# A gated two-layer block on one core: fewer weight units decoded ahead, another order of the first products, and token folds in the downs

## Chip, cores and metric

One core of a Trainium2 chip (trn2) runs the whole kernel. The metric is the device time of one execution in microseconds; the median of three runs is quoted.

## What is computed

Eight sequences of 256 tokens with 1024 features pass through four residual updates, each on a layer norm of the stream and scaled by the tanh of a gate: linear attention, a feed-forward net with 4-bit weights, an auto-correlation attention, and a linear layer with a column norm. The change touches the first two.

```python
x = x + tanh(g_xattn[0]) * linear_attention(layernorm(x), ctx, ctx)
x = x + tanh(g_ffn[0])   * ffn(layernorm(x))
x = x + tanh(g_xattn[1]) * autocorrelation(layernorm(x), ctx, ctx)
x = x + tanh(g_ffn[1])   * linear_with_norm(layernorm(x))

def ffn(x1):                    # DM = 1024, DFF = 2752, LoRA rank 16
    Wg, Wu, Wd = (NF4[codes] * absmax per block of 64, transposed)
    y1 = x1 @ Wg + x1 @ g_lora_a @ g_lora_b
    y2 = x1 @ Wu + x1 @ u_lora_a @ u_lora_b
    x3 = relu(y1) * y2
    return x3 @ Wd + x3 @ d_lora_a @ d_lora_b
```

## The kernel before, in words

**Phases.** `phase_linear_attention` (to 180 us of the span), `phase_nf4_ffn` (to some 1500 us), `phase_tail`. All engines run their own instruction lists in order and meet at semaphores. Matrices are split into a high and a low float16 part; a product is three matmuls (high x high, high x low, low x high).

**Linear attention.** Sixteen tiles of 128 tokens, one step each, with a few steps of lead and tail. In a step ScalarE copies transposed exponentials (L440), runs kinks of weight decoding (`first_kinks`, L424, instructions L434), spreads reciprocals (L446), takes the next tile's two exponentials (L413, L417), copies a PSUM tile (L452), normalises (L459) and casts a transposed tile (L422). POOL multiplies (L395) and computes reciprocal square roots (L386, L388). VectorE, among others, scales them (L525), makes the low half of a transposed tile (L539) and the reciprocal of sums (L549).

**Decoding.** The feed-forward weights come in units of 128 x 512 four-bit codes, as int32. A unit is decoded by eight Prelu operations on ScalarE in place, one per kink of a piecewise linear function. `AHEAD = 6` units are decoded in the linear attention: steps 1 to 8 run the eight kinks of units 0 to 2, one kink of each per step, and steps 9 to 16 those of units 3 to 5. Later ones go through `decode` (L1028), in two parts of four operations (instructions L1036).

**The feed-forward net.** DFF is padded to eleven pairs of two 128-row chunks c = 0, 1; a pass j handles a pair. A pass has gate and up products (A11, A12 are the two halves of the gate weights of a chunk, A21, A22 those of the up weights), then 32 downs, which multiply the hidden values with the down weights D0 to D3 and add into the stream X. Pass 0 does its products straight from the token tiles; from pass 1 on, products follow Strassen's scheme with seven products of combined operands. Their token combinations T1 to T4 are made once, in pass 0, for each of eight batches i (`fold_begin` on POOL L1309, two operations; `fold_first` L1658, three, and `fold_second` L1669, four, on VectorE; four casts `fold_hi` L1112, instructions L1118, on ScalarE; four `fold_lo` L1319, instructions L1323, on POOL), stored to DRAM (`x_parts`) and loaded back tile by tile.

**Steps of pass 0.** It has 24 steps, and every engine has a list for each (`first_step` at L1153 ScalarE, L1325 POOL, L1681 VectorE). Steps 0 to 15 are products: `first_products(n, m)` with s = 2n + m is 24 matmuls, for gate (m = 0) or up (m = 1) of turn n. `turn(n)` (L744) gives group g of tokens, chunk c, row half r. Turn n may begin when the hidden product of turn n - 2 is made (`hidden_first`, L1651, instruction L1656), since it takes over its PSUM banks. Steps 16 to 23 have four downs each. The 32 downs share six PSUM banks, and each waits until VectorE has accumulated the one that had its bank (`accumulate`, L1497, instruction L1501); the downs 4 and 5 wait for the last hidden product.

The list of VectorE in a step is short, and its order matters:

```python
if 0 < s <= 2 * TURNS and m == 1: hidden_first(n)
if folding(s): (fold_first, fold_second)[part](i)
for n in ...: accumulate(0, n)            # from step 16 on, four
for w in ended(0, s): weights(w)          # and lora_parts(1) after unit 11
```

ScalarE: ReLU of the turn (even m), a half decode, cast of units that ended a step before (`w_hi`, L1039, instruction L1055), cast of the hidden (odd m), casts of the fold, a second half decode where `halves` (L717) gives two. POOL: low parts of units (`w_lo`, L1255, instruction L1265), of the hidden (L1332), then the next batch's `fold_begin` and the low parts of the fold. `weights` (L1418) is two VectorE operations (L1439, L1442) and, for units of the next pass, one or two sums. `lora(w)` (L1730) is a small matmul in TensorE's order.

`halves(0, s)` is 1 in steps 0 to 15 and 1, 2, 1, 2, ... from 16 on; the units 6 to 19 are decoded there. `folding(s)` puts the two parts of batch i into steps 2i + 1 and 2i + 2, the last one into step 16. Units 0 to 3 are chunk 0, 4 to 7 chunk 1, 8 to 11 the downs of pass 0, 12 to 19 the gate and up units of pass 1.

**SyncE** issues all loads in order: per unit that ends, the load of unit w + 3 (L896), which waits until unit w has been scaled; the stores of folds; in step 18 the loads of token tiles 0 and 1 for pass 1, in step 20 those of tiles 2 to 4 (L909).

Of the kernel before, what the change touches and what calls it, by code (L numbers as in the profile page):

```python
# [20 lines left out]
I32 = mybir.dt.int32  # L21
# [6 lines left out]
B, L, D = 8, 256, 1024  # L28
# [13 lines left out]
HALVES = 2  # L42
UNITS = 12
CH = BANK // P
AHEAD = 6
LROWS = 96
GROUPS = 2
PRODUCTS = 7
# [528 lines left out]
def phase_nf4_ffn(nc, io, res):  # L577
# [11 lines left out]
    RING = 3  # L589
# [5 lines left out]
    TURNS = 4 * GROUPS  # L595
# [4 lines left out]
    with ExitStack() as ctx:  # L600
# [4 lines left out]
            return ctx.enter_context(nc.semaphore(name))  # L605

        lead = [res["first"][:, u, :] for u in range(AHEAD)]
        codes = [t.bitcast(I32) for t in lead[AHEAD - RING:AHEAD]]
        absm = [res["absm"][:, s, :] for s in range(RING)]
        level = lead[0:2]  # L610
        wt = [res["wt"][:, s, :] for s in range(4)]
# [102 lines left out]
        def steps(j):  # L714
            return ups(j) + DOWNS

        def halves(j, s):  # L717

            if j == 0:
                return 2 if s >= 2 * TURNS and s % 2 else 1  # L720
            if j == LAST_PASS:
                return 1 if s < 8 else 0
            return 2 if s in (14, 17) else 1
# [8 lines left out]
        def ended(j, s):  # L732

            return [w for w, part in decoded(j, s) if part]

        def earlier(j, s):

            return ended(j, s - 1) if s else ended(j - 1, steps(j - 1) - 1) if j else [4, 5]

        def sequence(j, g, p):  # L740

# [1 line left out]

        def turn(n):  # L744

            return n // 4, n // 2 % 2, n % 2

        def first_product(n, m):

# [29 lines left out]

        def all_hid(j, g):  # L780

            return (2 * j + g) * 4 + 4

        def folding(s):


            i, part = divmod(s - 1, 2)
            return (i, part) if 0 <= i < B else None

        def begun(i):  # L790

# [55 lines left out]
        for w in range(8 + LAST_PASS * UNITS + 4):  # L847
            j, u = unit_at(w)
# [44 lines left out]
        with nc.Block() as block:  # L893
            @block.sync
            def _(sp):
# [64 lines left out]
                for s in range(FIRST_STEPS):  # L960
                    if folding(s - 1):
                        i, part = folding(s - 1)
                        for k in range(2):
                            store_part(4 * i + 2 * part + k)
                    loads(0, s)
                    if 3 <= s < 3 + 3 * GROUPS:
                        store_block(s - 3)
                    if s == 2:
                        load_lora(1)
                    if s == 18:  # L970
                        for c in range(2):
                            sp.wait_ge(prod_mm[c], 4)
                        sp.wait_ge(blocks_out, 16 * 3 * GROUPS)
                        wait_parts(16)
                        for t in range(2):
                            load_x(t)
                    if s == 20:
                        for c in range(2):
                            sp.wait_ge(prod_mm[c], 8)
                        wait_parts(4 * B)  # L980
                        for t in range(2, XRING):
                            load_x(t)
                    if s == FIRST_STEPS - 1:
                        sp.wait_ge(hidlo_done, all_hid(0, 1))
                        for dst, name in zip(l_f, ("lora1_a", "lora1_b")):
                            sp.dma_start(dst, io[name]).then_inc(l_in, 16)
                for j in range(1, PAIRS):
                    if j < LAST_PASS:
                        load_lora(j + 1)
                    for s in range(steps(j)):  # L990
                        t = (j - 1) * UPS + s - 1 + XRING
                        if 0 < s <= UPS and t < LAST_PASS * UPS:
                            g, p = divmod(s - 1, PRODUCTS)
# [735 lines left out]
            def _(pe):  # L1729
                def lora(w):  # L1730


                    j, u = unit_at(w)
                    m, c, hf = units[u]
                    if u == 0:
                        pe.wait_ge(lb_done, j + 1)
                    if j == 0 and u in (0, 2, 8):
                        pe.wait_ge(la_done, m + 1)
                    if w > 1:
                        pe.wait_ge(wt_done, w - 1)  # L1740
                    o = ps_lora[w % 2]
                    if m == 2:
                        mm = pe.matmul(o[:], lora_b[:, m, c * P:(c + 1) * P], lora_a[:, m, hf * BANK:(hf + 1) * BANK], start=True, stop=True)
                    else:
                        for k in range(KD // 2):
                            kk = hf * (KD // 2) + k
                            mm = pe.matmul(o[:, k * P:(k + 1) * P], lora_a[:, m, kk * P:(kk + 1) * P], lora_b[:, m, c * P:(c + 1) * P], start=True, stop=True)  # L1747
                    mm.then_inc(lora_mm, 1)
# [193 lines left out]
                for s in range(FIRST_STEPS):  # L1942
                    if s < 2 * TURNS:
                        first_products(*divmod(s, 2))
                        if s == 0:
                            lora(4)
                            lora(5)
                        side(0, s)
                    else:
                        downs(0, s - 2 * TURNS)  # L1950
                for j in range(1, PAIRS):
                    for s in range(steps(j)):
                        g, p = divmod(s, PRODUCTS)
# [672 lines left out]
def build(nc, io):  # L2626
    with ExitStack() as ctx:
# [18 lines left out]
        for name, shape in (("a_st", [P, 2, 12]), ("a_mv", [P, 2, 2]), ("a_ve", [P, 2]), ("a_rstd", [P, 2]), ("a_nmr", [P, 2]),  # L2646
                            ("top8", [P, CH, 8]), ("next3", [P, CH, 8]), ("nmax", [P, CH]), ("wsum", [P, CH]), ("rws", [P, CH])):
            res[name] = sb(name, shape)
        for name, n in (("first", AHEAD), ("absm", 3), ("wt", 4)):
            res[name] = sb(name, [P, n, BANK])  # L2650
        res["made"] = sb("made", [P, 2, BANK], HALF)
        res["o_sp"], res["k_sp1"] = sb("o_sp", [P, 2, BANK]), sb("k_sp1", [P, 2, BANK])
# [122 lines left out]
```

## Time and profile before

| | |
|---|---|
| median of 3 runs | 2003.04 us (2002.95 to 2003.74) |
| the profiled execution, its own time | 2003.48 us |
| its span, first to last instruction | 2001.5 us |
| TensorE busy | 1918.8 us (96%) |
| VectorE busy | 1293.8 us (65%) |
| ScalarE busy | 1254.9 us (63%) |
| POOL busy | 835.4 us (42%) |

The profile gives for one execution the busy time of each engine, its idle time before an instruction with what released it, and a timeline. PE is TensorE's matmul, PEld its weight load, DVE VectorE, ACT ScalarE, SP SyncE. L12 is line 12 of the kernel. Matmuls overlap in the records: one of 512 columns shows 0.38 us, but a new one begins every 0.22 us at full clock.

### The profile page before, as it was taken

How to read it: one execution, taken by the hardware profiler on the slowest of the kernel's cores; microseconds unless marked ns; L12 is line 12 of the kernel's file. 1: busy time of each engine (PE TensorE's matmuls, PEld its weight loads, DVE VectorE, ACT ScalarE, POOL GpSimd, SP SyncE). 2: the span in 40 equal slices, each digit the busy share in tenths (PEclk: the TensorE clock that was granted, in tenths of full speed). 3: DMA queues.
4: the chain of work that ended last, by engine and by line, in shares of the span. 5: the costliest groups of instructions: out<-in, count | busy, mean ns of one | idle time of the engine just before them, and what ended most of it. 6: DMA issues, size and time to landing. Idle time of an engine off the chain costs nothing. (4 is left out here: it accounts for less than half of the span.)

```text
span 2001.5 us, 26467 instructions
## 1 busy us (share of the span) xinstructions
PE 1918.8 (96%) x9140; PEld 963.6 (48%) x9140; DVE 1293.8 (65%) x2204; ACT 1254.9 (63%) x1998; POOL 835.4 (42%) x752
## 2 busy tenths in 40 slices
PE   6996888999999999999999999999998899999998
PEld 5774334444444444444444445444444455555554
DVE  5776888364564736555473644636379988888872
ACT  6995668886777677676777776677524343443431
POOL 2443884222223223232232333222268667667742
PEclk9997998999999999999999999999999999999999
DMA  5651545856637375573737556373531110111001
GB/s 201 223 171 55 193 163 195 292 193 215 232 122 265 105 257 190 178 249 127 265 109 252 192 172 227 99 253 117 210 137 59 32 41 29 53 53 38 27 22 42
DMA packets 91989, 303.01 MB, mean 151 GB/s; under 512 B 11984, under 2 KB 16720, under 8 KB 73168
## 3 DMA queue, kind: packets, MB, share of 16 engines
q1 hardware_dynamic: 91856, 301.32, 44.3%
q8 instruction: 73, 1.20, 0.2%
q14 instruction: 60, 0.49, 0.1%
HBM read 274.01 MB, written 27.26 MB: 151 GB/s over the span
## 5 line engine op out<-in xcount | busy, mean ns | idle before, releaser
L1036 ACT ACTIVATE first<-first 128x512 f32<-128x512 int32 x1008 | 625.7, 626 | 27.4 <-DVE wt L1439 1.8
L1265 POOL TENSOR_TENSOR gu<-wt,gu 128x512 f16<-128x512 f32 x86 | 102.3, 1190 | 370.6 <-ACT gu L1055 370.5
L1439 DVE SCALAR_TENSOR_TENSOR wt<-first,w_scale,absm 128x512 f32<-128x512 f32 x132 | 102.6, 777 | 227.4 <-ACT first L1036 226.8
L1785 PE MATMUL a_psQ<-z,gu 128*128 128x512 f16 x936 | 208.5, 379 | 0.0
L2386 PE MATMUL a_psL<-z,l_x 128*128 128x512 f16 x768 | 170.7, 379 | 1.0 <-DVE l_x L2488 0.8
L1785 PE MATMUL a_psC<-z,gu 128*128 128x512 f16 x732 | 167.8, 379 | 0.0
L1785 PE MATMUL a_psC<-z 128*128 128x512 f16 x684 | 156.9, 379 | 0.0
L1785 PEld LDWEIGHTS a_psQ<-z,gu 128*128 128x128 f16 x936 | 91.5, 98 | 110.5
L1277 POOL TENSOR_TENSOR hid_lo<-z,hid_hi 128x512 f16<-128x512 f32 x76 | 90.2, 1201 | 118.7 <-ACT hid_hi L1096 118.6
L1265 POOL TENSOR_TENSOR dn_lo<-wt,dn_hi 128x512 f16<-128x512 f32 x42 | 50.3, 1197 | 199.2 <-ACT dn_hi L1055 199.2
L1442 DVE SCALAR_TENSOR_TENSOR wt<-a_psE,lora_gain,wt 128x512 f32<-128x512 f32 x132 | 99.1, 751 | 44.6 <-PE a_psE L1747 24.4
L2386 PEld LDWEIGHTS a_psL<-z,l_x 128*128 128x128 f16 x768 | 74.9, 98 | 89.1 <-issue 1.2
L1265 POOL TENSOR_TENSOR z<-wt,z 128x512 f16<-128x512 f32 x57 | 66.4, 1179 | 119.4 <-ACT z L1055 119.4
L1785 PEld LDWEIGHTS a_psC<-z,gu 128*128 128x128 f16 x732 | 70.7, 98 | 82.3
L1055 ACT ACTIVATE gu<-wt 128x512 f16<-128x512 f32 x86 | 53.4, 622 | 89.7 <-DVE wt L1442 78.5
L1501 DVE SCALAR_TENSOR_TENSOR X<-a_psL,ffn_gain,X 128x512 f32<-128x512 f32 x132 | 94.9, 744 | 19.8 <-PE a_psL L1838 19.7
L1785 PEld LDWEIGHTS a_psC<-z 128*128 128x128 f16 x684 | 66.4, 98 | 78.8
L1838 PE MATMUL a_psL<-dn_hi,hid_hi 128*128 128x512 f16 x268 | 101.6, 379 | 1.4 <-DVE X L1501 1.4
L1785 PE MATMUL a_psL<-z 128*128 128x512 f16 x456 | 101.7, 379 | 0.0
L1838 PE MATMUL a_psL<-dn_hi,hid_lo 128*128 128x512 f16 x268 | 101.5, 379 | 0.0
L1501 DVE SCALAR_TENSOR_TENSOR X<-a_psQ,ffn_gain,X 128x512 f32<-128x512 f32 x106 | 77.8, 746 | 36.8 <-PE a_psQ L1838 36.8
L1501 DVE SCALAR_TENSOR_TENSOR X<-a_psC,ffn_gain,X 128x512 f32<-128x512 f32 x108 | 78.6, 746 | 31.1 <-PE a_psC L1838 30.9
(418 smaller groups left out, 4122.3 us busy)
## 6 DMA issues: line engine op xcount, KB each, us to landing
z<-x_parts SPq DMA_DIRECT2D x140, 1024.0 KB, 5.8
first<-in_codes SPq DMA_DIRECT2D x132, 256.0 KB, 3.0
absm<-in_absmax SPq DMA_DIRECT2D x264, 128.0 KB, 3.3
X<-in_x SPq DMA_DIRECT2D x16, 512.0 KB, 4.3
c_in<-in_ctx SPq DMA_DIRECT2D x16, 512.0 KB, 5.3
cT<-in_ctxT SPq DMA_DIRECT2D x16, 512.0 KB, 3.6
o_sp<-in_w SPq DMA_DIRECT2D x16, 512.0 KB, 4.8
z<-in_ctx SPq DMA_DIRECT2D x8, 1024.0 KB, 7.0
```

What stands on the lines that cost most here:

```text
L1036: act.activation(level[w % 2][:], codes[w % RING] if k == 0 else level[w % 2][:], ACT.Prelu, bias=bias, scale=scale, alpha=alpha).then_inc ...
L1055: act.activation(dest(c, name, 0), wt[slot(name)], ACT.Copy).then_inc(whi_done, 1)
L1265: pool.tensor_tensor(low, source, high, ALU.subtract).then_inc(wlo_done, 1)
L1277: pool.tensor_tensor(low, buf, high, ALU.subtract).then_inc(hidlo_done, 1)
L1439: dve.scalar_tensor_tensor(wt[at], source[:], w_scale[:, m:m + 1], absm[w % RING][:], ALU.mult, ALU.mult).then_inc(scaled, 1)
L1442: dve.scalar_tensor_tensor(wt[at], ps_lora[w % 2], lora_gain[:, m:m + 1], wt[at], ALU.mult, ALU.add).then_inc(wt_done, 1)
L1501: dve.scalar_tensor_tensor(dst, ps_ring[down_bank(j, n)], ffn_gain[:], dst, ALU.mult, ALU.add).then_inc(acc_done, 1)
L1785: mm = pe.matmul(out, w[:, k * P:(k + 1) * P], xx[:, k], start=first and q == 0, stop=q == 3 * KD // 2 - 1, skip_group_check=True)
L1838: mm = pe.matmul(ps_ring[down_bank(j, n)], hh[c][:, i * P:(i + 1) * P], w[c][:, hf * BANK:(hf + 1) * BANK], start=(q == 0), stop=(q == len ...
L2386: mm = pe.matmul(sum_bank(d, half), a[:, ks], w[:, k, half * CB:(half + 1) * CB], start=(q == 0), stop=(q == 3 * KD - 1))
```

## The change

Four units instead of six are decoded in the linear attention, two in steps 1 to 8 and two in steps 9 to 16; units 4 to 19 are decoded in pass 0, two halves in steps 6 and 12 and from 18 on. The buffer `first` keeps six slots, and codes of later units use slots 3 to 5. The turns of pass 0 run over all tokens with chunk 0 and then with chunk 1. The parts of the folds lie in two of three steps up to 14 and in steps 16 to 21. The loads of tiles 2 to 4 move from step 20 to step 22, and the LoRA matmuls of units 4 and 5 from step 0 to steps 1 and 3.

```diff
-AHEAD = 6
+AHEAD = 4
+FIRST_SLOTS = 6
...
-        codes = [t.bitcast(I32) for t in lead[AHEAD - RING:AHEAD]]
+        codes = [res["first"][:, u, :].bitcast(I32) for u in range(FIRST_SLOTS - RING, FIRST_SLOTS)]
...
         def halves(j, s):
             if j == 0:
-                return 2 if s >= 2 * TURNS and s % 2 else 1
+                return 2 if s in (6, 12) or s >= 18 else 1
...
         def earlier(j, s):
-            return ended(j, s - 1) if s else ended(j - 1, steps(j - 1) - 1) if j else [4, 5]
+            return ended(j, s - 1) if s else ended(j - 1, steps(j - 1) - 1) if j else []
...
         def turn(n):
-            return n // 4, n // 2 % 2, n % 2
+            return n // 2 % 2, n // 4, n % 2
...
         def all_hid(j, g):
-            return (2 * j + g) * 4 + 4
+            return (2 * j + g) * 4 + 4 if j else 6 + 2 * g
...
         def folding(s):
-            i, part = divmod(s - 1, 2)
-            return (i, part) if 0 <= i < B else None
+            order = [t for t in range(1, 16) if t % 3] + list(range(16, 22))
+            return divmod(order.index(s), 2) if s in order else None
...
-                    if s == 20:
+                    if s == 22:
                         for c in range(2):
                             sp.wait_ge(prod_mm[c], 8)
                         wait_parts(4 * B)
...
                     if s < 2 * TURNS:
                         first_products(*divmod(s, 2))
-                        if s == 0:
-                            lora(4)
-                            lora(5)
                         side(0, s)
...
-        for name, n in (("first", AHEAD), ("absm", 3), ("wt", 4)):
+        for name, n in (("first", FIRST_SLOTS), ("absm", 3), ("wt", 4)):
```

## Rows read from the trace of the kernel before

**Rows 1.** Busy time by stretch: start:end, length, busy and count per engine, TensorE clock, DMA.
```profile
75.00:175.00 100.00, 85.41 (x582) 68.90 (x580) 74.14 (x151) 88.39 (x111) 39.43 (x49) 0.98 0.44 144
203.00:304.00 101.00, 81.99 (x367) 35.84 (x365) 85.86 (x80) 65.44 (x114) 84.51 (x60) 0.93 0.49 176
346.30:446.30 100.00, 100.00 (x483) 45.98 (x482) 48.67 (x70) 80.61 (x138) 27.69 (x25) 1.00 0.72 241
```
**Rows 2.** Timeline of TensorE, pass 0: start, length, instruction, [idle before, releaser].
```profile
200.81 10.53 PE L1806 MATMUL a_psC<-z,gu 128*128 128x512 f16 x48
...
227.50 4.97 PE L1806 MATMUL a_psQ<-z,gu 128*128 128x512 f16 x12 [6.91 <-POOL gu L1265]
...
278.01 0.40 PE L1747 MATMUL a_psE<-lora_b,lora_a 96*128 96x128 f16 x4 [3.02 <-DVE lora_b L1416]
...
304.67 0.61 PE L1838 MATMUL a_psC<-dn_hi,hid_hi 128*128 128x512 f16 x1 [8.24 <-DVE gain_row L1656]
...
311.21 0.39 PE L1838 MATMUL a_psL<-dn_hi,hid_hi 128*128 128x512 f16 x1 [1.24 <-DVE X L1501]
...
346.25 5.34 PE L1785 MATMUL a_psQ<-z,gu 128*128 128x512 f16 x24
```
**Rows 3.** Timeline of ScalarE, POOL and VectorE in one step of the linear attention.
```profile
87.18 1.00 ACT L452 ACTIVATE wt<-psB 128x1024 f32<-128x1024 f32 x1
...
91.08 1.66 ACT L434 ACTIVATE first<-first 128x512 f32<-128x512 f32 x3
93.27 1.06 ACT L446 ACTIVATE wt<-made 128x1024 f32<-128x1024 f32 x1 [0.52 <-DVE made L549]
...
88.26 2.36 POOL L395 TENSOR_TENSOR eq<-wt,eq 128x1024 f32<-128x1024 f32 x1 [0.44 <-ACT wt L452]
...
91.49 0.16 DVE L525 SCALAR_TENSOR_TENSOR made<-made 128x1 f32<-128x1 f32 x1 [0.79 <-POOL made L388]
...
92.83 0.34 DVE L549 RECIPROCAL made<-psB 128x32 f32<-128x32 f32 x1
```
**Rows 4.** Timeline of ScalarE: L446 in steps 2 and 15.
```profile
37.35 1.05 ACT L446 ACTIVATE wt<-made 128x1024 f32<-128x1024 f32 x1
...
160.25 1.05 ACT L446 ACTIVATE wt<-made 128x1024 f32<-128x1024 f32 x1
```
**Rows 5.** Timeline of VectorE in pass 0.
```profile
211.85 0.74 DVE L1656 SCALAR_TENSOR_TENSOR gain_row<-a_psQ,hid_gain,gain_row 128x512 f32<-128x512 f32 x1
...
242.82 1.52 DVE L1679 TENSOR_TENSOR first<-first,z 128x512 f32<-128x512 f32 x1
...
248.10 0.75 DVE L1439 SCALAR_TENSOR_TENSOR wt<-first,w_scale,absm 128x512 f32<-128x512 f32 x1 [0.86 <-ACT first L1036]
...
252.14 0.69 DVE L1673 TENSOR_TENSOR o_sp<-o_sp,z 128x512 f32<-128x512 f32 x1 [1.84 <-POOL k_sp L1323]
...
303.87 0.74 DVE L1656 SCALAR_TENSOR_TENSOR gain_row<-a_psC,hid_gain,gain_row 128x512 f32<-128x512 f32 x1
...
344.62 1.40 DVE L1501 SCALAR_TENSOR_TENSOR X<-a_psC,ffn_gain,X 128x512 f32<-128x512 f32 x2
```
**Rows 6.** Timeline of ScalarE in pass 0.
```profile
196.66 2.62 ACT L1036 ACTIVATE first<-first 128x512 f32<-128x512 int32 x4 [1.40 <-DMA first<-in_codes]
...
245.40 2.60 ACT L1036 ACTIVATE first<-first 128x512 f32<-128x512 f32 x4
...
249.24 0.63 ACT L1118 ACTIVATE k_sp<-o_sp 128x512 f16<-128x512 f32 x1 [0.72 <-DMA x_parts<-k_sp]
```
**Rows 7.** Timeline of POOL in pass 0.
```profile
249.83 2.28 POOL L1323 TENSOR_TENSOR k_sp<-o_sp,k_sp 128x512 f16<-128x512 f32 x2
252.97 1.61 POOL L1265 TENSOR_TENSOR dn_lo<-wt,dn_hi 128x512 f16<-128x512 f32 x1 [0.86 <-ACT dn_hi L1055]
```
**Rows 8.** SyncE's timeline in pass 0, then the DMA issues of the page (count, size, us to landing).
```profile
329.55 1.42 SPq L909 DMA_DIRECT2D z<-x_parts  x3
...
z<-x_parts SPq DMA_DIRECT2D x140, 1024.0 KB, 5.8
```

## The prediction

> **What bounds the kernel now.** I read the busy time by stretch first, then each engine in order of time where the change touches it. From 346.3 us on TensorE has no idle time [rows 1]: whatever moves the start of pass 1 (346.25 us, [rows 2]) moves the end by as much. So the question is when pass 0 ends. Two stages come before. In the first phase (to 180 us) ScalarE looks like the bound, busy 88 of 100 us [rows 1]. In pass 0 TensorE waits 6.91, 3.02 and 8.24 us [rows 2], each time for work of the other three engines, and VectorE is idle only 15.1 of 101 us [rows 1].
>
> **First phase: one kink fewer per step (L424).** Is ScalarE's kink work on the path? In one step ScalarE ends its three kinks and then still waits 0.52 us for the reciprocal L549 [rows 3]. Follow that wait back: L549 follows L525, which waits for POOL's L388, which stands behind the product L395 (2.36 us), which waits for ScalarE's L452 at 87.18 [rows 3]. From L446 on ScalarE runs without idle to the next L452. This ring makes the step of 9.3 us, and the kinks lie beside it: without one of them (1.66 / 3, some 0.5 us) the wait becomes 1.0 us and nothing is gained. Only in steps 2 and 15 does L446 start right behind the kinks, with no wait shown [rows 4]: 2 x 0.5 = **-1.0 us**. Bounds: 0, and 16 x 0.5 = -8.3 if my ring is wrong.
>
> **How pass 0 is costed.** TensorE does a product turn (two steps) in 10.6 us [rows 2], sixteen steps in 85. I lay out VectorE, ScalarE and POOL in the order of their step lists: an operation starts when its engine is free and its wait is met. Prices: half a decode 2.6 us on ScalarE, a cast 0.55; on VectorE a unit's weights 1.5 (two operations of 0.75), a hidden product 0.7, an accumulation 0.66 in a row; a combination operation 0.69 alone and 1.53 while POOL runs [rows 5, 6]; on POOL 1.15 alone, 1.6 beside VectorE [rows 7]. I write h0 to h7 for the hidden products L1656, which TensorE waits for two turns later; the last two feed the downs.
>
> **Start of pass 0.** The 1.40 us wait for codes [rows 6] goes, since the codes of unit 4 are asked for two units earlier, and two casts of units 4 and 5 leave (1.1 us). h0, which ended at 212.6 [rows 5], ends at 209.8. The weights of units 4 and 5 (3.0 us of VectorE) and four decode halves (10.4 us of ScalarE) come in behind it. The 6.91 us wait for the low part of unit 7 goes: chunk 1 is first needed in step 8, not 4. What is late next is the hidden product of two turns before.
>
> **Steps 2 to 16 by hand.** Steps 2 and 3: combination ends 213.4; ScalarE has by then decoded only half of unit 5, its second half ends 217.2; weights, then h1 at 219.4. Steps 4 and 5: first combination to 222.3; in POOL's list the low parts of unit 5 and of h1 (3.0), the next batch's two first operations (2.4) and two low parts (2.3) stand ahead of the second combination, so VectorE waits until 228.1, 5.8 us with nothing in its list between (before, weights and a hidden product stood there and 1.84 us was left [rows 5]). Second combination 231.4, weights 233.6, h2 at 234.3: TensorE, ready at 232.2, waits 2.1. Steps 6 to 9: unit 7 is ready only at 238.3 (two halves and two casts from 232.0), weights 239.8, combination 241.9, h3 242.6; wait for POOL to 248.0; combination 252.5, weights, h4 at 255.4. So six steps take 36 us against TensorE's 31.8. Steps 10 to 12: combination 258.0, unit 9 ready at 259.3 and its weights 260.9, wait for POOL to 266.0, combination 270.5, h5 at 271.2 (TensorE, ready at 267.2, waits 4.0). Steps 12 to 16: both halves of unit 10 or 11 fall into step 12, so its list is one half longer; unit 10's weights 275.2, combination 277.5, unit 11's weights 281.4, the next pass's LoRA rows some 284.0, h6 at 284.7; POOL's low parts to 286.9, combination 290.9; ScalarE then has two casts, a ReLU and half of unit 12, to 294.5; weights 296.0, h7 **296.7**, where it was 304.6 [rows 5]. The low half of D3 (unit 11), decoded only in step 13, is ready at 288.1, so the downs start there, not at 291.1; they stop at the fifth for h7. Products thus gain 8 us.
>
> **The downs.** Three batches now lie here (21 combination operations, before 4), in VectorE's list ahead of each step's accumulations, and TensorE can run only six banks ahead of those. From h7 to accumulation 25, which frees the bank of the last down, VectorE has 21 combinations (at 1.1, midway, since POOL has work for about half of that stretch, 25 operations of 1.15: 23), 26 accumulations (17.2), weights of units 13 to 17 (7.5), five sums (3.5), and waits for POOL's low parts in the first pair (some 4): 55.6 us. So accumulation 25 ends at 352.3, the last down 1.5 us later, 353.8 against 346.25: **+7.5 us**. Bounds: all 21 at 0.69 (-8.6), all at 1.53 (+9.0). ScalarE keeps up: 10 halves, 12 and 9 casts are 37.6 us there.
>
> First the row: combinations take 0.69 or 1.53 us, and POOL's operations 1.15 or 1.6, as the other runs or not [rows 5, 7]. The Trainium skill, SBUF — State Buffer, "SBUF: two separate sides", says why: a VectorE operation with two SBUF inputs and a GpSimd operation take an exclusive lock in turn, and the loser blocks for the whole instruction. By that rule the stretch from h7 to accumulation 25 holds 25 POOL operations (28.8 us) and 31 such VectorE operations (21.4), 50.2 us at least, so an end of pass 0 at 348.4 even with every other wait gone; put in place of the 55.6 it gives 2004.6 us. The trace agrees in the two values that each operation takes.
>
> **Pass 1.** SyncE's load of tiles 2 to 4 moves from step 20 to 22, and there it stands behind unit 21's load, which waits for unit 18's first scaling (some 355). Before, it was issued at 329.55 [rows 8]. Issue at 357 and 5.8 us to landing, three side by side some 7: 364, and product 2 wants them at 364.4. I take **+0.5 us**; bounds 0 and 3. Loads of tiles 0 and 1 keep step 18, and the folding of tokens 0 to 3 ends in step 11, well ahead. all_hid(0, 0) = 6 costs nothing: h5 ends 17 us before the downs.
>
> **Sum.** -1.0 + 7.5 + 0.5 = +7.0 us on the profiled execution (2003.48 us, span 2001.5). That execution is 0.44 above the median of the runs shown, which I take as the base: 2003.0 + 7.0 = **2010.0 us**. A measurement of this kernel tells some 0.2%, 4 us, from no change.
>
> **Rivals.**
> Faster: the waits of VectorE do not grow. Its work up to accumulation 25 is the same but for units 4 and 5; my layout is longer by some 14 us of waits, most of them at the second combination. If POOL gets through the two first operations of the next batch (2.4 us) while VectorE is still in its own three, that gap shrinks by 2.4 in five product batches and in the first downs pair: 14.4 us, 1995.6. It decides from 1.2 us per batch on. For it: POOL is relieved of a third of its folds, 84.5 us busy in 101 [rows 1]. Against: low parts of units and hiddens stand ahead of them, behind ScalarE's decodes. Chance 0.27, from 1994 to 1999.
> No difference: ScalarE does bound the first phase, as its 88% suggest; all sixteen steps shrink, 7.3 us more than in the sum: 2002.7. Against: the 0.52 us wait in every steady step. With the cases that end between the two others by chance, 0.22.
> Slower still: TensorE's clock. After its 6.91 us of waiting, 12 matmuls took 4.97 us, twice the usual [rows 2], the half clock of 1.2 GHz. If it stays there through downs that starve, a step of 24 takes 9.9 us, and 28 downs 69 instead of 57: 2022. The Trainium skill, TensorE: Matmul & The Clock Gate, Part 1, calls the throttled clock the default that activity releases. Against: in the first phase the granted clock is 0.98 with TensorE busy 85 of 100 us [rows 1]. Chance 0.06.
> Forecast, slower: 0.45.
>
> **Numbers.** The forecast's own range, 2006 to 2018, comes from the price of combinations in the downs and from h7 5 us earlier or later. With the faster rival the range is 1994 to 2020. Faster 0.27, same 0.22, slower 0.51.
>
> **What would show it.** Right: first-phase step still 9.3 us with the wait before L446 near 1.0; no TensorE wait for a low part of chunk 1 around step 5; h7 near 296; TensorE in the downs waiting for X (L1501) again and again, where it waited 1.24 us once [rows 2]; VectorE near 90% busy from 297 to 352; pass 1 beginning near 353. Wrong: a first-phase step of 8.8 us; or VectorE waiting under 2 us at each second combination and pass 1 beginning before 346; or TensorE waiting for z at product 2 by more than 3 us.

## The result, and the profile after

The changed kernel takes **2027.87 us** (median of 4 runs, 2025.03 to 2030.49), the kernel before 2003.39 beside it (4 runs); ratio 1.0119, 95% interval 1.0101 to 1.0136. Slower by 24.5 us: the forecast's side, but 17.9 us above 2010.0 and outside the range. The profiled execution took 2030.49 us (span 2028.7, against 2001.5). Code lines of the feed-forward part are one higher than before (L1656 is now L1657).

Busy time of the changed kernel by stretch, columns as in [rows 1]. The second line runs from the first hidden product to the last (h0 to h7), the third from the start of h7 to the end of accumulation 25:

```profile
75.00:175.00 100.00, 85.89 (x575) 68.86 (x574) 73.40 (x150) 82.50 (x100) 39.45 (x49) 0.96 0.43 144
208.73:297.73 89.00, 77.55 (x343) 33.77 (x341) 49.05 (x58) 61.97 (x107) 50.01 (x42) 0.92 0.50 181
297.73:360.98 63.25, 41.07 (x183) 17.71 (x184) 50.10 (x65) 38.47 (x66) 34.30 (x26) 0.87 0.39 123
363.20:463.20 100.00, 93.56 (x440) 42.36 (x439) 46.02 (x65) 77.91 (x133) 27.59 (x24) 0.97 0.78 263
```

The products are shorter (h0 to h7 took 92.0 us before), the downs much longer: the third stretch took 36.0 us before. Pass 1, whose first 100 us were 100% busy [rows 1], now has 6.4 us without TensorE.

TensorE's timeline in the changed kernel, which answers to [rows 2]:

```profile
243.31 2.76 PE L1807 MATMUL a_psQ<-z,gu 128*128 128x512 f16 x12 [1.19 <-POOL gu L1266]
...
271.34 13.16 PE L1807 MATMUL a_psC<-z,gu 128*128 128x512 f16 x48 [3.89 <-DVE gain_row L1657]
...
311.57 0.61 PE L1839 MATMUL a_psC<-dn_hi,hid_hi 128*128 128x512 f16 x1 [3.91 <-DVE X L1502]
...
331.82 0.61 PE L1839 MATMUL a_psL<-dn_hi,hid_hi 128*128 128x512 f16 x1 [6.97 <-DVE X L1502]
...
345.24 0.61 PE L1839 MATMUL a_psC<-dn_hi,hid_hi 128*128 128x512 f16 x1 [6.43 <-DVE X L1502]
...
363.21 5.34 PE L1786 MATMUL a_psQ<-z,gu 128*128 128x512 f16 x24
...
385.65 4.56 PE L1786 MATMUL a_psC<-z 128*128 128x512 f16 x12 [6.43 <-ACT z L1074]
```

Pass 1 starts at 363.21, 17.0 us later than at 346.25 [rows 2]. From its start to the end of the span are 1665.5 us (2028.7 - 363.21), where they were 1655.3: 10.2 more. The two make the span's 27.2. In the downs TensorE waits again and again for X, that is for VectorE's accumulations. What does VectorE wait for? Its timeline there:

```profile
297.73 0.74 DVE L1657 SCALAR_TENSOR_TENSOR gain_row<-a_psC,hid_gain,gain_row 128x512 f32<-128x512 f32 x1
...
306.99 0.69 DVE L1674 TENSOR_TENSOR o_sp<-first,z 128x512 f32<-128x512 f32 x1 [2.99 <-POOL k_sp L1324]
...
322.39 1.20 DVE L1440 SCALAR_TENSOR_TENSOR wt<-first,w_scale,absm 128x512 f32<-128x512 f32 x1 [1.20 <-ACT first L1037]
...
339.37 0.75 DVE L1440 SCALAR_TENSOR_TENSOR wt<-first,w_scale,absm 128x512 f32<-128x512 f32 x1 [5.63 <-ACT first L1037]
...
348.40 0.75 DVE L1440 SCALAR_TENSOR_TENSOR wt<-first,w_scale,absm 128x512 f32<-128x512 f32 x1 [1.25 <-ACT first L1037]
...
357.40 0.75 DVE L1440 SCALAR_TENSOR_TENSOR wt<-first,w_scale,absm 128x512 f32<-128x512 f32 x1 [1.21 <-ACT first L1037]
...
359.58 1.40 DVE L1502 SCALAR_TENSOR_TENSOR X<-a_psL,ffn_gain,X 128x512 f32<-128x512 f32 x2
...
362.93 0.75 DVE L1440 SCALAR_TENSOR_TENSOR wt<-first,w_scale,absm 128x512 f32<-128x512 f32 x1 [0.63 <-ACT first L1037]
```

Accumulation 25 is the second of the pair at 359.58. Four of the five units' weights before it wait for ScalarE's kinks (9.3 us in all), the longest 5.63. One step further back, ScalarE's timeline (L1119 is the cast of a folded part into one of three stage buffers, which must first have been stored to DRAM):

```profile
319.15 0.63 ACT L1119 ACTIVATE k_sp<-o_sp 128x512 f16<-128x512 f32 x1 [2.23 <-DMA x_parts<-k_sp]
319.69 5.10 ACT L1037 ACTIVATE first<-first 128x512 f32<-128x512 f32 x8
...
328.01 0.63 ACT L1119 ACTIVATE made<-o_sp 128x512 f16<-128x512 f32 x1 [1.01 <-DVE o_sp L1676]
336.10 0.63 ACT L1119 ACTIVATE k_sp<-o_sp 128x512 f16<-128x512 f32 x1 [7.46 <-DMA x_parts<-k_sp]
336.64 5.10 ACT L1037 ACTIVATE first<-first 128x512 f32<-128x512 f32 x8
...
354.13 0.63 ACT L1119 ACTIVATE k_sp<-o_sp 128x512 f16<-128x512 f32 x1 [2.20 <-DMA x_parts<-k_sp]
...
383.88 1.05 ACT L1135 ACTIVATE o_sp<-gain_row 32x1024 f32<-32x1024 f32 x1 [7.07 <-DMA k_sp<-in_lora_b]
```

Two things are to be seen. The eight kinks (5.10 us) start each time right behind the two casts, so what holds a cast holds the next weights. And the casts wait for stores: 2.23, 7.46, 1.83 (at 345.14) and 2.20, together 13.7 us. Why is a store late? SyncE's timeline:

```profile
323.61 0.33 SPq L903 DMA_DIRECT2D first<-in_codes  x1
323.99 1.11 SPq L905 DMA_DIRECT2D absm<-in_absmax  x2
325.36 0.85 SPq L910 DMA_DIRECT2D z<-x_parts  x2
326.25 1.57 SPq L949 DMA_DIRECT2D x_parts<-k_sp  x2
...
365.38 1.40 SPq L910 DMA_DIRECT2D z<-x_parts  x3
...
372.06 0.60 SPq L987 DMA_DIRECT2D gain_row<-in_lora_a  x1
372.69 0.43 SPq L987 DMA_DIRECT2D k_sp<-in_lora_b  x1
```

The stores of 326.25 (256 KB each) stand behind a unit's load, which waits for a `scaled` of VectorE, and behind tiles 0 and 1, 2 MB; the cast is let go at 336.10, 9.9 us after their issue. Their usual time to landing, and that of the factor rows behind tiles 2 to 4 (3 MB), stands in the DMA view of 300 to 400 us (KB each, median us to landing):

```profile
x_parts<-k_sp SPq DMA_DIRECT2D x8, 256.0 KB, 3.4
...
gain_row<-in_lora_a SPq DMA_DIRECT2D x1, 384.0 KB, 8.8
k_sp<-in_lora_b SPq DMA_DIRECT2D x1, 384.0 KB, 11.2
```

The rows asked for at 372.69 let ScalarE go at 383.88, and behind L1135 on ScalarE stands the snapshot L1074 that TensorE waits 6.43 us for. (A snapshot is ScalarE's copy of a product out of PSUM, which frees the bank.) The 12 matmuls after that wait took 4.56 us at a granted clock of 0.58; in a4_folds_back (below) they took 2.75 us, at 1.00, after a wait of 0.51 us.

### The profile page after: what moved, and what is told of

Same layout as the page of the kernel before. It is cut to its first block and busy times, and to the rows that moved or that the text cites. A ratio compares the mean times of both kernels' runs of the same rounds, so it can differ in the third digit from the quotient of the medians.

```text
span 2028.7 us, 26469 instructions
## 1 busy us (share of the span) xinstructions
PE 1928.5 (95%) x9140; PEld 966.4 (48%) x9140; DVE 1277.7 (63%) x2204; ACT 1256.1 (62%) x1998; POOL 824.4 (41%) x752
## 5 line engine op out<-in xcount | busy, mean ns | idle before, releaser
L1037 ACT ACTIVATE first<-first 128x512 f32<-128x512 f32 (+1 forms) x1024 | 635.4, 626 | 26.3 <-DVE wt L1440 1.8
L1266 POOL TENSOR_TENSOR gu<-wt,gu 128x512 f16<-128x512 f32 x86 | 103.8, 1207 | 385.8 <-ACT gu L1056 385.8
L1266 POOL TENSOR_TENSOR dn_lo<-wt,dn_hi 128x512 f16<-128x512 f32 x42 | 48.7, 1160 | 209.5 <-ACT dn_hi L1056 209.5
L1839 PE MATMUL a_psL<-dn_lo,hid_hi 128*128 128x512 f16 x254 | 97.8, 385 | 0.0
```

The lines of the kernel that those rows point to most:

```text
L1037: act.activation(level[w % 2][:], codes[w % RING] if k == 0 else level[w % 2][:], ACT.Prelu, bias=bias, scale=scale, alpha=alpha).then_inc ...
L1266: pool.tensor_tensor(low, source, high, ALU.subtract).then_inc(wlo_done, 1)
L1839: mm = pe.matmul(ps_ring[down_bank(j, n)], hh[c][:, i * P:(i + 1) * P], w[c][:, hf * BANK:(hf + 1) * BANK], start=(q == 0), stop=(q == len ...
```

## The experiments

Theory A: the folds in the downs cost what they cost because ScalarE's casts wait for late stores; the factor rows behind tiles 2 to 4 are a second cost, of its own. Rival B: two more units decoded in pass 0 are the loss. C and D came later. All results in one table: median; first to last hidden product; last hidden product to accumulation 25 (the downs); start of pass 1; from there to the end of the span. "4" and "6" are the units decoded ahead.

```
                     median   h0-h7  downs  pass 1   rest
before (6)          2003.39    92.0   36.0  346.25  1655.3
after (4)           2027.87    89.0   63.3  363.21  1665.5
b6_order            2004.38    92.4   36.0  345.45  1655.3
b6_order_folds      2019.52    82.4   57.6  355.64  1660.5
a4_folds_back       2009.39   105.1   38.7  355.15  1657.7
a4_factors_first    2020.33    89.2   63.1  360.26  1657.3
a4_tiles_early      2022.50    88.7   58.1  357.45  1662.3
a4_stores_now       2021.01    88.7   57.2  354.75  1664.1
a4_both             2014.00    88.7   58.4  358.92  1655.8
a4_sums_first       2033.56    88.8   69.8  371.19  1662.6
a4_casts_last       2019.53    89.7   56.2  355.48  1661.8
a4_cure             2013.47    88.7   57.1  358.69  1655.2
a4_cure_casts       2012.03    88.7   54.7  354.36  1657.0
a4_cure_short       2002.91    88.6   45.4  345.71  1656.3
b6_cure             2006.84    94.3   37.7  349.22  1656.9
a4_cure_back        2010.16   103.8   38.7  350.58  1656.9
b6_folds_cure       2006.98    81.7   53.2  349.07  1655.9
a4_mix_cure         2007.11    91.8   47.8  346.19  1656.3
b6_mix_cure         2003.01    85.9   42.0  345.60  1655.2
```

The median is the result; the stretches are of one execution, whose start to first product differs by some 2 us either way between kernels with the same first phase. That of a4_folds_back took 2014.61 us, 5.2 above its median. The kernel before, measured beside each group of kernels, had medians from 2003.39 (beside the result) to 2005.24 us (beside the next four), so a difference between kernels of two groups can be off by some 2 us.

### The change in parts

**a4_folds_back**: the changed kernel with the old folding steps and tiles 2 to 4 loaded at step 20 again.

```diff
-            order = [t for t in range(1, 16) if t % 3] + list(range(16, 22))
-            return divmod(order.index(s), 2) if s in order else None
+            i, part = divmod(s - 1, 2)
+            return (i, part) if 0 <= i < B else None
```

> The changed kernel, but with the folds in steps 1 to 16 and the loads of tiles 2 to 4 in step 20, as before. Theory A (the folds in the downs are what costs: VectorE waits for them with accumulations behind, and the late tile loads hold up the factor rows): pass 1 begins between 346 and 352 us instead of 363.2, no 6.4 us wait in pass 1, 2002 to 2009 us. Rival B (the two units decoded in pass 0 cost it, 10.4 us of ScalarE): pass 1 still begins after 357 us, 2014 to 2022.

2009.39 us, ratio 1.003 (1.0017 to 1.0043): almost as theory A expected. Pass 1 began at 355.15 in its profiled execution, between what A and B expected. **b6_order**: the kernel before with the new order only.

```diff
-            return n // 4, n // 2 % 2, n % 2
+            return n // 2 % 2, n // 4, n % 2
...
-            return (2 * j + g) * 4 + 4
+            return (2 * j + g) * 4 + 4 if j else 6 + 2 * g
```

> The kernel before with only the order of the turns changed (chunk 0 over all tokens first). Both theories: the 6.9 us wait for unit 7 goes, but the hidden products stay bound by VectorE's list, so h7 stays within 3 us of 304.6 and the time within 4 us of 2003. A third theory C, that the order itself costs (the last downs' hidden products crowd at the end), expects more than 2008.

2004.38 us, ratio 0.9996 (0.9987 to 1.0006): the order alone is free. Its trace loses the 6.91 us wait of [rows 2], and pays it back in four waits for hidden products (0.9 to 2.5 us) and 1.1 us more at the LoRA rows. **b6_order_folds**: the same with the new folding steps and later tiles.

```diff
-            i, part = divmod(s - 1, 2)
-            return (i, part) if 0 <= i < B else None
+            order = [t for t in range(1, 16) if t % 3] + list(range(16, 22))
+            return divmod(order.index(s), 2) if s in order else None
...
-                    if s == 20:
+                    if s == 22:
```

> Six units decoded ahead as before, new order of turns, folds spread into the downs and tiles 2 to 4 loaded in step 22. Theory A: nearly the whole loss is there, 2018 to 2026 us, with a wait for the factor rows in pass 1 above 4 us. Rival B: without the two extra units the loss is under half, 2003 to 2012.

2019.52 us, 1.0076 (1.006 to 1.0093). So folds in the downs cost 15.1 us with six units ahead and 18.5 with four (2027.87 - 2009.39); four units ahead cost 5 us with the old folds and 8.4 with the new. Set against the kernel before beside each, the 18.5 and the 8.4 are some 2 us larger. Either way the folds are the larger part, B the smaller.

**a4_factors_first**: the two factor loads (L987) at step 22, ahead of tiles 2 to 4, not in the last step.

```diff
                         wait_parts(4 * B)
-                        for t in range(2, XRING):
-                            load_x(t)
-                    if s == FIRST_STEPS - 1:
                         sp.wait_ge(hidlo_done, all_hid(0, 1))
                         for dst, name in zip(l_f, ("lora1_a", "lora1_b")):
                             sp.dma_start(dst, io[name]).then_inc(l_in, 16)
+                        for t in range(2, XRING):
+                            load_x(t)
```

> The changed kernel with the two loads of factor rows (lora1_a, lora1_b) issued in step 22 ahead of the loads of tiles 2 to 4, not after unit 22's load in step 23. Theory A2 (ScalarE's 7.1 us wait for these rows and TensorE's 6.4 us behind it come from 3 MB of tiles ahead of them in the queues): the wait in pass 1 falls under 1 us and the slow clock after it goes, 2018 to 2021 us. Rival: the snapshots are late anyway since ScalarE is behind at the end of pass 0, then 2025 to 2028.

2020.33 us: -7.5. The rows asked for second land 5.8 us after their issue, not 11.2. The 6.43 us wait in pass 1 is gone, the rest of the span is 1657.3 instead of 1665.5, the downs are as long as before.

### The stores

**a4_tiles_early** and **a4_both** (the same with the factors first):

```diff
-                    if s == 18:
+                    if s == 15:
```

> The changed kernel with tiles 0 and 1 of pass 1 (two loads of 1 MB) issued three steps earlier on SP (step 15, not 18), ahead of the downs instead of in their third step. Theory A (ScalarE's fold casts wait for stores of parts that stand behind those 2 MB and SP's unit load, and the downs' accumulations stand behind the folds): the wait of 7.46 us at 336 us falls to about 2, the two long waits of TensorE for X (6.97 and 6.43 us) lose about 6 us together, pass 1 starts at 356 to 359 us instead of 363.2, and the time falls by 4 to 7 us, to 2021 to 2024. Theory B (the folds' own work on VectorE, ScalarE and GpSimd is the length of the downs, stores only take the blame): pass 1 starts where it did and the time stays within 2 us of 2028.

> The changed kernel with tiles 0 and 1 issued at step 15 and the two factor loads of pass 1 issued ahead of tiles 2 to 4. If the two costs are separate (stores behind tiles 0 and 1 in the downs; factor rows behind tiles 2 to 4 in pass 1) they add: 7.5 us as measured with the factors alone, and the 4 to 7 us of the tiles: 2013 to 2017. If the one only moved the other's wait, the time is that of the better of the two alone, about 2020.

2022.50 and 2014.00: -5.4 and -13.9, which is the sum of the two within 1 us. **a4_stores_now** stores a part in the step that makes it, ahead of that step's unit load:

```diff
-                    if folding(s - 1):
-                        i, part = folding(s - 1)
+                    if folding(s):
+                        i, part = folding(s)
```

> The changed kernel with SP storing the parts of a fold in the step that makes them and ahead of that step's unit load, where they now wait for the step's unit load in the queue. Theory A has two causes for a late store: the queue's unit load ahead of it, and the bytes ahead of it. If the queue matters, ScalarE's three waits of about 2 us go, with 2 to 4 us of the time; the 7.46 us behind tiles 0 and 1 stays. If bytes alone matter, the time stays within 1 us of 2028. It can also turn slower, where SP's wait for a fold delays a unit load and with it a decoded unit.

2021.01: -6.9, more than the 2 to 4 expected, and no wait of ScalarE for a store is left in the downs. The expectation had the 7.46 us wait stay; but the move takes its store ahead of tiles 0 and 1 too (issued at 318.24, the tiles at 321.65), so for this wait the run does not part the place in the queue from the bytes ahead. The other three, 6.3 us in all, had only a unit's load in front: for them the place in SyncE's queue was enough. Yet the downs still took 57.2.

**a4_sums_first** puts `accumulate` ahead of the fold in VectorE's step of the downs.

```diff
+                    for n in range((s - 2 * TURNS) * PER_STEP, (s - 2 * TURNS + 1) * PER_STEP) if s >= 2 * TURNS else ():
+                        accumulate(0, n)
                     if folding(s):
...
-                    for n in range((s - 2 * TURNS) * PER_STEP, (s - 2 * TURNS + 1) * PER_STEP) if s >= 2 * TURNS else ():
-                        accumulate(0, n)
```

> The changed kernel with VectorE's accumulations of a downs step ahead of the fold part of that step, not behind it. Theory A (the accumulations are late because they stand behind folds that wait for ScalarE and the stores): TensorE's waits for X shrink to that of the first step or so, accumulation 25 ends 8 to 12 us earlier than 361.0, and the time falls by 5 to 10 us even though every store is as late as before; what can remain is that tiles 2 to 4 are loaded later, as the folds end later. Theory B (VectorE's own work in a step is what counts, in whatever order): acc 25 within 2 us of 361 and 2026 to 2030 us.

2033.56, 5.7 **slower**: the expectation fell, and with it the thought that accumulations are late because they stand behind folds. ScalarE's timeline in this kernel:

```profile
318.27 0.63 ACT L1119 ACTIVATE k_sp<-o_sp 128x512 f16<-128x512 f32 x1 [2.93 <-DVE o_sp L1662]
321.39 0.63 ACT L1119 ACTIVATE k_sp<-o_sp 128x512 f16<-128x512 f32 x1 [2.49 <-DVE o_sp L1668]
321.93 5.10 ACT L1037 ACTIVATE first<-first 128x512 f32<-128x512 f32 x8
```

Casts now wait for folds that stand behind the accumulations, and the kinks start that much later. It is a ring: weights (VectorE), folds (VectorE), casts (ScalarE), kinks (ScalarE), weights. An accumulation ahead of the folds lies in the ring, behind them beside it. In the trace the step from one unit's weights to the next grew from 9.0 us (339.37, 348.40, 357.40) to 11.5 and 11.2 (341.25, 352.77, 364.01), most of the 2.8 us of accumulations moved; the time grew by less than all such steps, since ScalarE's waits for stores fell from 13.7 to 5.0 us. This is theory C.

**a4_casts_last** opens the ring on ScalarE:

```diff
+                    for w, part in pieces[1:] if s >= 2 * TURNS else ():
+                        decode(w, part)
                     if folding(s):
...
-                    for w, part in pieces[1:]:
+                    for w, part in pieces[1:] if s < 2 * TURNS else ():
```

> The changed kernel with ScalarE's two fold casts of a downs step behind that step's kinks, not ahead of them. The trace of the changed kernel shows a ring in the downs: VectorE's weights wait for ScalarE's 8 kinks (5.10 us), the kinks stand behind two casts, the casts behind VectorE's folds, and the folds behind VectorE's weights: 9.0 us from one step's weights to the next where no store is badly late (339.37, 348.40, 357.40), against 5.5 in the step without a fold (357.40, 362.93). Theory C (that ring is a cost of its own, beside the late stores): with the kinks ahead, a step takes 7 to 8 us, ScalarE's waits for stores fall beside VectorE's folds, and the time falls by 4 to 9 us, to 2019 to 2024. Theory A alone (only the late stores stretch the downs): the stores are as late, and the time stays within 2 us of 2028.

2019.53: -8.3, downs 56.2, with SyncE's order untouched. ScalarE still waits 5.4 us for one store, but VectorE's waits for the kinks up to accumulation 25 fell from 9.3 to 0.8 us. So the late stores hurt mainly through the kinks behind them. **a4_cure** is all three moves on SyncE, **a4_cure_casts** those and the casts behind the kinks.

> The changed kernel with all three moves on SP: parts stored in their own step, tiles 0 and 1 at step 15, factor loads ahead of tiles 2 to 4. Tiles and factors together gave 2014.0, stores alone 7 us of 2028. The tiles and the stores take away the same waits in part (ScalarE's stores waited 13.7 us in all, of which the tiles' move left 6.1): theory A expects 4 to 5 us more than the two moves, 2009 to 2010.5, with no wait of ScalarE for a store in the downs. What is left over the kernel before (some 5 to 6 us) is then the ring of folds, kinks and weights, and fewer units decoded ahead.

> The three moves on SP, and the casts behind the kinks. Theory C: 3 to 6 us less than with the three moves alone, 2003 to 2007, near the kernel before. Without C: the same as the three moves alone, within 2 us.

2013.47 and 2012.03: both miss, and prompt stores on top of a4_both (2014.00) give nothing that the measurement can tell. The cures of the downs do not add: early tiles, prompt stores and late casts each take away the same 5 to 7 us, and below some 55 us the downs do not go. VectorE in the last of these kernels:

```profile
333.29 0.69 DVE L1459 TENSOR_TENSOR wt<-wt 128x512 f32<-128x512 f32 x1
333.90 0.68 DVE L1663 TENSOR_TENSOR first<-first,z 128x512 f32<-128x512 f32 x1
334.61 1.53 DVE L1667 TENSOR_TENSOR o_sp<-z,first 128x512 f32<-128x512 f16 x1
336.17 1.53 DVE L1669 TENSOR_TENSOR o_sp<-o_sp,z 128x512 f32<-128x512 f32 x1
337.63 1.40 DVE L1503 SCALAR_TENSOR_TENSOR X<-a_psC,ffn_gain,X 128x512 f32<-128x512 f32 x2
338.95 1.39 DVE L1503 SCALAR_TENSOR_TENSOR X<-a_psL,ffn_gain,X 128x512 f32<-128x512 f32 x2
340.27 0.73 DVE L1441 SCALAR_TENSOR_TENSOR wt<-first,w_scale,absm 128x512 f32<-128x512 f32 x1
```

No gap between one step's weights and the next, and none from 306.12 to 351.53. **a4_cure_short** tests that VectorE is the bound (theory D): the 21 combinations of the downs work on 32 columns of 512, and the rest of them is left out, so this kernel computes something else.

```diff
-                        (fold_first, fold_second)[part](i)
+                        (fold_first, fold_second)[part](i, 32 if s >= 2 * TURNS else BANK)
```

> As the three moves on SP and the casts behind the kinks, but VectorE's 21 fold instructions of the downs work on 32 of 512 columns (so tokens' combinations are left out in part; this only measures). Theory D (VectorE's own work bounds the downs of that kernel: busy 50.8 of 54.7 us, without a gap from 306.1 to 351.5): 21 instructions lose about 0.6 us each, and more where they took 1.5; the downs fall by 12 to 16 us to some 40 us, where ScalarE's 5.5 to 7 us a step take over, and the time to about 1998 to 2000. If something else bounds them, the downs shorten by less than 5 us.

2002.91: -9.1 us, downs 45.4, above the 1998 to 2000 and the some 40 expected. VectorE is busy 39.6 us there, 11.2 less than the 50.8 before, and the downs are 9.3 shorter: D holds. The gain is smaller than expected, since a wait of 4.48 us for POOL and some dear short combinations stay (below). **b6_cure** is the kernel before with the factors first and tiles 0 and 1 earlier:

```diff
-                    if s == 18:
+                    if s == 11:
```

> The kernel before with tiles 0 and 1 loaded seven steps earlier and the factor loads ahead of tiles 2 to 4. There no part is stored in the downs, TensorE is busy all through the first 100 us of pass 1, and ScalarE's only wait that these loads could cause is 2.4 us at the factors: both theories expect no measurable change, 2001 to 2005. Tiles 0 and 1 ahead of the stores of the last parts could cost 1 to 3 us.

2006.84, ratio 1.0009 (0.9999 to 1.0018): above the expected 2001 to 2005, and nothing to win there.

### What is left, and a split

**a4_cure_back** is a4_folds_back with the three moves on SyncE, **b6_folds_cure** is b6_order_folds with these and late casts. **a4_mix_cure** is a4_cure_casts with three fold parts in the downs, not six:

```diff
-            order = [t for t in range(1, 16) if t % 3] + list(range(16, 22))
+            order = [t for t in range(1, 16) if t not in (6, 12)] + list(range(16, 19))
```

> Four units ahead with the folds back in the products' steps and the three moves on SP. Folds back alone: 2009.4, downs 38.7 us, products 105 us from first to last hidden product (before 92). If late stores also stretched its products (ScalarE waited 17.5 us for them there), the time falls to 2004 to 2007; if four units ahead is the whole of its loss, it stays at 2008 to 2010.

> Six units ahead, the new order, folds in the downs, and all moves of the cured kernel (stores, tiles, factors, casts). Without them it was 2019.5. Theory D gives downs near VectorE's busy time (48.4 us plus some 3) where they were 57.6, and 3.4 us less in pass 1: 2007 to 2011. So folds in the downs alone would cost 3 to 6 us over the kernel before.

> The cured kernel with three fold parts in the downs instead of six: three more in steps 3, 9 and 15 of the products. Theory D: the downs lose 3 times VectorE's 2.9 to 4.5 us, some 10 us; the products gain 3 parts' share (six parts cost them 16 us between the two layouts: some 8 us). Time 2008 to 2012, near the cured kernel's 2012.

2010.16, 2006.98 and 2007.11 (ratios 1.003, 1.0013, 1.0012); the last is 0.9 below its expected range. The first says that four units ahead with the folds back lose nothing by late stores: ScalarE waited 17.5 us for them in a4_folds_back, none here, and the time is the same. With the cures, folds in the downs cost 1.9 us with four ahead (2012.03 - 2010.16), which is within the intervals of the two, and nothing with six (2006.98 against 2006.84), where they cost 18.5 and 15.1 without. Four units ahead cost 3.3 us with the folds back (2010.16 against b6_cure's 2006.84) and 5.1 with the folds in the downs. Three fold parts in the downs have the lowest median with four ahead; **b6_mix_cure** is the same with six:

> Six units ahead, new order, the moves on SP and the casts behind the kinks, three fold parts in the downs (six in b6_folds_cure, 2007.0; none before, 2004.4). If the optimum lies between, as with four ahead (3 to 5 us below both ends), 2000 to 2003 and faster than the kernel before. If VectorE's and ScalarE's work in these two stretches is the limit in whatever split, 2004 to 2007.

2003.01 against 2004.07, ratio 0.9995 (0.9986 to 1.0004): level with the kernel before, not faster, and at the edge of the 2000 to 2003 that a best split in between would have given.

## Why the prediction was wrong, point by point

**First phase: right.** The step is still 9.32 us, and ScalarE's wait behind the kinks is the predicted 1.0:

```profile
83.22 1.06 ACT L447 ACTIVATE wt<-made 128x1024 f32<-128x1024 f32 x1 [1.05 <-DVE made L550]
92.54 1.06 ACT L447 ACTIVATE wt<-made 128x1024 f32<-128x1024 f32 x1 [1.05 <-DVE made L550]
```

ScalarE's busy share fell from 88 to 82.5%, and hardly anything was gained by it. The first product starts at 185.7 us in the mean of the 13 kernels with four units ahead (183.5 to 187.8) and at 186.7 in the mean of the 6 with six: -1.0, the predicted term, though within the spread of single executions. The rival by which ScalarE bounds this phase is out.

**Products: right.** The hidden products ended at 209.5, 219.4, 233.9, 242.9, 254.8, 271.3, 284.4 and 298.5; the layout by hand had 209.8, 219.4, 234.3, 242.6, 255.4, 271.2, 284.7 and 296.7. (The layout leaves out the first phase's -1.0 us, which the sum adds on its own; with it h7 was forecast at 295.7 and pass 1 at 352.8.) VectorE's waits for POOL at the second combination were 5.63, 4.97, 4.85 and 2.49 us, where the layout had 5.8, 5.4, 5.1 and 2.2, and the wait for unit 7's low part shrank from 6.91 to 1.19 us. The faster rival, which lived on POOL getting through its list in time, is out. The low half of D3 came at 288.0 (288.1).

**Downs: the first step that failed.** From the end of h7 to accumulation 25 it took 62.5 us, not 55.6. VectorE's own work was sized rightly: the 21 combinations took 21.5 us (1.02 each, 1.1 predicted), weights 8.0 (7.5). Wrong was "ScalarE keeps up". Its sum of 37.6 us of work was right, 38.5 busy from the start of h7, but it is not free to do that work when it is due: kinks stand behind casts, and casts wait for folds and for stores. VectorE waited 9.3 us for kinks beside 3.0 for POOL, where the layout had some 4 in all. With h7 1.8 us late and 0.7 more behind accumulation 25, pass 1 started at 363.2, not 353.8. VectorE was busy 43.1 of the 55 us from 297 to 352, 78% and not near 90%. The stores were never followed through SyncE's queue: the prediction names its loads of tiles 0 and 1 as harmless because their sources are ready, and never asks what stands behind them.

**Pass 1: the second step that failed; right place, wrong size and wrong instruction.** Predicted +0.5 us, bounds 0 and 3, for tiles 2 to 4. TensorE waited for no tile. It waited for a snapshot behind ScalarE's L1135, which waits for factor rows that SyncE issues behind those tiles; before, the same wait was 2.4 us at 358.02 and hidden. The rest of the span was 10.2 us longer in this execution (1665.5 against 1655.3), of which a4_factors_first gives back 8.2, and 7.5 in the medians. What the factor loads stand behind was put at nothing without a reason: the prediction does not name them.

Of the profiled execution's surplus over the forecast, some 20 us (the span grew by 27.2, not 7.0), 10.4 came before pass 1 and 9.7 from its start on. Curing one of the two failed steps alone leaves the time above the range's 2018 (2019.53 to 2022.50); a4_both, with both, has 2014.00.

**Slower still by the half clock.** The clock in the downs was 0.87 of full, but TensorE waited there for VectorE, and shorter waits alone brought the time back; the clock was not the cause. In a4_cure_casts, with downs 8.6 us shorter, the granted clock there was 0.88. In pass 1 the half clock of 1.2 GHz after the 6.43 us wait is a part of the 8.2 us: 1.8 us in the 12 matmuls shown.

**The lock as floor.** Combinations still take 0.69 or 1.53 us, and with the waits gone VectorE is the bound of the downs (a4_cure_casts, 54.7 us from the start of h7, 53.9 from its end). The lock of the Trainium skill, SBUF — State Buffer, "SBUF: two separate sides", had given a floor of 50.2 us from the end of h7, an estimate. No run with all 21 combinations whole in the downs went below it, but none shows that it is what binds: in a4_cure_casts VectorE's whole list, busy 50.8 us, fills the stretch by itself. The changed kernel stayed 12 us above that floor, for the reason given.

Two sums are slightly off and change nothing: the terms of the downs add up to 55.2, not 55.6, and 16 x 0.5 is 8.0, not 8.3.

By the numbers: 7.0 us forecast, 24.5 measured. Late stores and the ring carry 5.4 to 8.3 us of the medians, the factor rows 7.5; together 13.9 (a4_both) to 15.8 (a4_cure_casts). The 7.8 us that are left (2012.03 against the 2004.26 of the kernel before beside it) are near the 7.0 forecast, which had priced VectorE's work and little else; but that is in part luck, for 5.1 of them go with four units ahead (against b6_folds_cure), where the forecast had put +7.5 on the downs. Not tried was a fourth stage buffer, and not settled is why four units ahead cost 3.3 us with the folds back and all waits for stores gone; the table only says where, in the products (103.8 us in a4_cure_back, 94.3 in b6_cure).

## What to carry to other kernels

Moving work past a point of an engine's list moves its DMAs past everything in the issuing queue too: follow each store to whoever waits for its buffer, and ask what is queued behind a bulk load, not only whether its source is ready. An engine that has idle time in sum still doesn't keep up if its work stands behind waits; look for a ring (who waits for whom in one step, back to the start), for work inside the ring costs nearly its full time (2.2 to 2.5 of 2.8 us a step in a4_sums_first), and the same work beside it much less. Where several cures take away the same wait, each alone looks like the whole cause; run them together before adding them up, and look for the engine that has no gap left.

## What was not expected of the hardware

- A VectorE combination that competes with POOL paid about the same here whatever its own size, not a multiple. In a4_cure_short the same instruction on 32 columns takes 0.19 us alone and 1.08 beside POOL (+0.89); on 512 columns it is 0.69 and 1.53 (+0.84). VectorE's rows, then POOL's beside them:

```profile
319.92 1.14 DVE L1675 TENSOR_TENSOR o_sp<-o_sp,z 128x32 f32<-128x32 f32 x1
321.09 1.08 DVE L1677 TENSOR_TENSOR o_sp<-o_sp,z 128x32 f32<-128x32 f32 x1
...
336.11 0.19 DVE L1677 TENSOR_TENSOR first<-first,z 128x32 f32<-128x32 f32 x1
...
319.41 2.71 POOL L1267 TENSOR_TENSOR z<-wt,z 128x512 f16<-128x512 f32 x2
322.08 1.15 POOL L1267 TENSOR_TENSOR gu<-wt,gu 128x512 f16<-128x512 f32 x1
```

  The second of these combinations ends at 322.17, POOL's pair at 322.12; so the price may well be the rest of POOL's instruction, 1.15 us or so each. No run changed the size of POOL's operations, so this is not shown.

- A 256 KB store lands in 3.4 us (median) but was waited for until 9.9 us after its issue behind 2 MB of loads. The 384 KB of rows took 11.2 us behind 3 MB of tiles and 5.8 ahead of them (a4_factors_first): in these runs the bytes issued ahead on the queue were paid first.
